# LSTM and three dense layers on one core: the last sixteen time steps as two portions of eight

## What is computed

```python
xW = einsum('ntd,dg->ntg', x, Wx) + b          # n=32, t=64, d=256, g=1024
def step((h, c), xw_t):
    a = xw_t + h @ Wh                          # Wh 256 x 1024
    i, f, o = sigmoid(a[:, :768] in three);  g = tanh(a[:, 768:])
    c = f * c + i * g
    h = o * tanh(c)
hs = scan(step)                                # 64 steps, one after the other
y = s0 * ([hs, -hs] @ pm1(k0))                 # 512 -> 1024
y = s1 * ((relu(y) * 2) @ pm1(k1))             # 1024 -> 1024
y = s2 * ((relu(y) * 2) @ pm1(k2))             # 1024 -> 256
out = x + y
```

## Time and profile before

| | |
|---|---|
| median of three runs | 282.81 us |
| the profiled execution | 282.9 us |
| its span (first to last instruction) | 281.1 us |
| TensorE busy | 275.7 us (98%) |
| VectorE busy | 203.1 us (72%) |
| ScalarE busy | 158.3 us (56%) |
| TensorE's granted clock | full in every slice |

### The profile page before, as it was taken

The page is one execution under the profiler, slowest core; times in us unless marked ns, Lnnn a source line. Parts: engine busy times, 40 slices in busy tenths (PEclk is TensorE's granted clock), DMA queues, the critical chain, the costliest instruction groups (busy, mean ns, idle before and its releaser), DMA issues.

```text
span 281.1 us, 8774 instructions
## 1 busy us (share of the span) xinstructions
PE 275.7 (98%) x3608; PEld 223.5 (80%) x3608; DVE 203.1 (72%) x747; ACT 158.3 (56%) x480; POOL 2.3 (1%) x10
## 2 busy tenths in 40 slices
PE   8899999999999999999999999999999999999995
PEld 5688888777998989999899999999999895544441
DVE  2787888887788888887888888788887875431113
ACT  5596987787656556565555566655566454211100
POOL 0100000000000000000000000000000000000000
PEclk9999999999999999999999999999999999999999
DMA  6960000000000001000100010000000100010001
GB/s 191 398 277 1 3 2 0 2 3 0 2 2 3 3 2 40 2 2 3 40 1 2 3 40 2 2 2 22 22 2 2 40 3 0 0 37 2 0 0 75
DMA packets 4791, 8.72 MB, mean 31 GB/s; under 512 B 912, under 2 KB 2448, under 8 KB 4624
## 3 DMA queue, kind: packets, MB, share of 16 engines
q1 hardware_dynamic: 4176, 7.87, 7.8%
q10 hardware_dynamic: 576, 0.30, 0.4%
HBM read 6.07 MB, written 2.10 MB: 29 GB/s over the span
## 4 chain that ended last, share of the span: by engine, by line
PE 90%; DVE 3%; DMA 3%; ACT 1%; SPq 1%; issue 0%; DVEq 0%
PE WK L396 48%; PE WK L379 14%; PE G L359 10%; PE ACC L409 9%; PE G L350 9%; DMA xw<-in_wh 3%; ACT tT L543 1%; DVE h L592 1%; DVE x L597 1%; DVE mx L574 0%; DVE aT L703 0%; SPq L315 0%; ACT tC L548 0%; DVE cD L714 0%; DVE uT L712 0%
## 5 line engine op out<-in xcount | busy, mean ns | idle before, releaser
L396 PE MATMUL WK<-h,k 128*128 128x256 f16 (+1 forms) x992 | 126.7, 276 | 0.1
L396 PEld LDWEIGHTS WK<-h,k 128*128 128x128 fp8e5 x992 | 93.6, 98 | 15.5 <-issue 1.6
L543 ACT ACTIVATE tT<-aT 128x128 f32<-128x128 f32 x126 | 39.0, 310 | 57.8 <-DVE aT L703 56.5
L592 DVE SCALAR_TENSOR_TENSOR h<-WK,h 128x256 f16<-128x256 f32 (+1 forms) x104 | 42.4, 439 | 27.2 <-ACT h L504 27.2
L504 ACT ACTIVATE h<-WK 128x256 f16<-128x256 f32 (+1 forms) x104 | 37.1, 388 | 30.0 <-PE WK L396 29.8
L703 DVE TENSOR_REDUCE aT<-G 128x128 f32<-128x256 f32 x128 | 48.2, 418 | 6.8 <-PE G L359 5.9
L486 ACT ACTIVATE G<-xw 128x256 f32<-128x256 f32 x126 | 46.6, 370 | 0.0
L379 PE MATMUL WK<-xs,wxs 128*128 128x512 f32 x168 | 43.7, 403 | 0.7 <-DVE wxs L570 0.7
L359 PE MATMUL G<-h,w 128*128 128x64 f16 x1008 | 39.5, 192 | 0.0
L350 PEld LDWEIGHTS G<-h,w 128*128 128x128 f16 x1008 | 32.6, 96 | 6.3 <-DVE h L720 4.0
L409 PE MATMUL ACC<-h,k 128*128 128x256 f16 (+1 forms) x224 | 36.5, 288 | 0.1
(11 more groups left out here) (63 smaller groups left out, 132.8 us busy)
## 6 DMA issues: line engine op xcount, KB each, us to landing
x<-in_x SPq DMA_DIRECT2D x3, 512.0 KB, 8.9
out_y<-x SPq DMA_DIRECT2D x12, 128.0 KB, 1.8
xw<-in_wx SPq DMA_DIRECT2D x4, 256.0 KB, 5.9
xw<-in_wh SPq DMA_DIRECT2D x4, 256.0 KB, 7.0
k<-in_k SPq DMA_DIRECT2D x1, 1024.0 KB, 10.8
k<-in_k SPq DMA_DIRECT2D x1, 512.0 KB, 8.3
out_y<-x SPq DMA_DIRECT2D x2, 256.0 KB, 2.0
x<-in_x ACTq DMA_DIRECT2D x1, 256.0 KB, 4.3
```

The source lines that it names most:

```text
L396: ins = eng.matmul(layer_src(tile), w, rhs, start=a == 0, stop=last)
L543: eng.activation(tT[:, B * j0:B * j1], aT[:, j0:j1].rearrange("p j b -> p (j b)"), ACT.Tanh, scale=half_gain0 if t == 0 else half_gain).th ...
L592: eng.scalar_tensor_tensor(layer_dst(tile, 1), layer_src(tile), 0.0, layer_dst(tile, 0), ALU.max, ALU.subtract).then_inc(lo_made[tile[0]])
```

## The change

`CHUNKS` gets eight portions of 8 steps in place of six of 8 and one of 16. `third` is called for every portion, so that the first-layer tiles of portions 6 and 7 stand beside the second-layer tiles of portions 5 and 6 as those of the earlier portions do, and the special order for the last portion goes. The first-layer outputs of portions 6 and 7 share the space of the former portion 6, half each, and the rule of when ScalarE may write there is extended to both.

```diff
-LAST = 2
-CHUNKS = ((0, 8), (8, 8), (16, 8), (24, 8), (32, 8), (40, 8), (48, 16))
+CHUNKS = ((0, 8), (8, 8), (16, 8), (24, 8), (32, 8), (40, 8), (48, 8), (56, 8))
@@ tile_order
-            if c < NC - 2:
-                order += third(c, m)
-        if c == NC - 2:
-            rest = [(tile, 1) for tile, n in order[-LAST:] for _ in range(n)]
-            del order[-LAST:]
-            share = len(rest) // 8
-            for n in range(8):
-                order += [((0, c + 1, n), 4)] + rest[share * n:share * n + share]
-            order += rest[8 * share:]
+            order += third(c, m)
     return order + [(("o", NC - 1, k), 2) for k in (6, 7, 6, 7)]
@@ lstm_ffn
         h1s = [f.rearrange("p (m a c) -> p m a c", m=8, a=2) for f in (
-            h1[:, 0:4096], h1[:, 4096:8192], h1[:, 0:4096], h1[:, 4096:8192], h1[:, 0:4096], h1[:, 4096:8192], h1b)]
+            h1[:, 0:4096], h1[:, 4096:8192], h1[:, 0:4096], h1[:, 4096:8192], h1[:, 0:4096], h1[:, 4096:8192], h1b[:, 0:4096], h1b[:, 4096:8192])]
@@ layer_hi
-                if layer == 0 and 2 <= c < NC - 1:
+                if layer == 0 and 2 <= c < NC - 2:
                     e.wait_ge(l_mm[1], 8 * (c - 1))
-                if layer == 0 and c == NC - 1:
+                if layer == 0 and c >= NC - 2:
                     e.wait_ge(seeded[1], 16)
```

## The result

The changed kernel takes 283.22 us (median of 22 runs, 282.56 to 283.90); the kernel before took 282.70 beside it (22 runs, 282.14 to 283.20). The ratio is 1.0020, with a 95% interval of 1.0013 to 1.0026: slower by 0.57 us, between 0.37 and 0.74 (the medians alone differ by 0.52). The forecast was 283.0 us, and 282.4 to 283.7 as the range.

The account below looks back on a forecast made before the run. The prediction took the kernel as bound by the columns TensorE streams, plus late steps and the end. Its terms, 1.73 + 0.17 - 1.47 - 0.2 = +0.23 us, gave 283.0 us, with 282.4 to 283.7 as the 8-in-10 range.

Parts of the forecast that it names:

- What bounds the kernel: Whole kernel: the columns TensorE streams, plus some tenths where a step is late, plus the end; no gap in 44.96 us.
- Two narrow for a wide: Last portions' matmuls: 192 wide become 384 narrow at 0.1091 us, +0.46; stretch after the last step +1.73 us.
- The straight line between the two spacings: TensorE matmul price: 81 ns at 128 columns and 131 at 512 give 98 at 256, costing 12.5 us; prediction rejected it.
- Steps 59 and 60: VectorE's queue: three pieces behind each step put h 3.52 us apart, so step 62 starts late, +0.17 us.
- from step 62 on h needs 3.12 again and is early: Steps from 62: h comes every 3.12 us again, so TensorE does not wait for it there.
- Behind the last step: Filling after step 63: no gap to win; banks return in 2.73 us against about 1.0 of emptying; cost nothing.
- B: Behind the last step: banks come back late, ten tiles wait 0.20 us each, +2.0, to 285.0 us; chance 0.08.
- E: Long narrow streams run slower than the fills: each 0.01 us more is 3.8 us, 286.8 us; chance 0.02.
- The end: From the last twelve output matmuls on: smaller pieces win back 1.47 us, the smaller last transfer 0.2 us.
- A: Steps with three VectorE pieces cost nearly nothing, 0.04 us each: 282.8 us; chance 0.13.
- C: Small terms at upper bounds: narrow at 0.1094 (+0.13), transfer unchanged (+0.2), steps +0.25: 283.4 us; chance 0.12.

## Why the prediction was right, and where it was short

- *What bounds the kernel.* Right: the stretch from the last step to the last twelve output matmuls is a count of matmuls, 46.72 us for a forecast of 46.69, and TensorE waits nowhere in it.
- *Two narrow for a wide.* Forecast 0.46; measured alone 0.45 for 360, so 0.48 for 384. The straight line between the two spacings of the Trainium skill ("TensorE: Matmul & The Clock Gate", section "Back-to-back issue gap") would have asked for an estimated 12.5 us; the traces don't agree, with 216 ns at 512 columns and 109 at 256.
- *Steps 59 and 60.* The mechanism was right and its first part exact: the h of steps 60 and 61 were forecast for 222.15 and 225.67 and are there then (221.93 and 225.45, each 0.22 long), and step 62 was forecast at 225.72 and stands at 225.74. The term of 0.17 was too small. The step of the reasoning that failed is "from step 62 on h needs 3.12 again and is early": the low part of the h of step 61 was not early, a stall of VectorE's own fell on the float32 h that it is made from, and TensorE waited 0.14 us within step 62. The whole term is 0.32 to 0.33 us: step 60 to step 63 takes 10.35 to 10.36 in three traces of the changed order and 10.03 before. No row of before shows it at step 61, but the idle 0.47 of step 22 stood in the trace, and I had not looked for such rows.
- *Behind the last step.* Nothing was lost and nothing won, as forecast; rivals B and E did not occur.
- *The end.* Forecast -1.67, measured -1.62 in the span: from the last twelve to the next matmul that waited there were 1.10 us, for 1.04. The gap behind the six covering matmuls, 0.44 us, is real and closed when ten covered. The transfer is shorter by 0.23 us in the span (2.27 for 2.50), for -0.2 forecast; but the forecast took the time outside the span as unchanged, and there it grew by about as much on average.
- *The rivals.* A (the crowded steps cost nearly nothing) holds for the first of the two, which cost 0.04 (3.31 us to step 61), and fails for the second (3.53 to step 62). C is the nearest to what came, but not by its terms: narrow cost 0.1091 and the transfer was shorter.
- *The forecast as a whole* has the direction and the parts right, and half of the size: +0.45 us in the trace for +0.23 forecast, with 0.14 missing for the stall, 0.05 at the end and 0.03 in the stretch. The timed loss of 0.57 is more than twice the forecast one, and the term that it had not looked at is the one outside the span. That 283.22 us lies so near to the forecast 283.0 is in part luck: the kernel before was timed at 282.70 this time and not at 282.81, and counted from there the forecast is 0.3 low. The 0.71 for a change within 0.2% is neither won nor lost: the ratio of 1.0020 lies on that border.

## What to carry to other kernels

Where an engine is full, as TensorE is here, cutting its work finer costs its price (here 1.2% of what was cut) and pays at the end alone, where the last emptying, the last y piece and its transfer are smaller; but less work is left to cover that emptying, so count the matmuls that cover it before and after. When tiles are moved into a loop with a recurrence, count the instructions that each engine holds ahead of the recurrence's next one: two steps in a row with three were costlier than the one with three before. And when starts vary from run to run, compare traces from the first instruction of the loop; waits of 0.1 us in a single step can then be read, which the times don't part. Take beside it the time outside the span for every execution: a change can move that too.

## What the runs showed of the hardware

VectorE stalled at two fixed places of its instruction stream, by 0.14 to 0.25 us, and in the same place in every trace of the same stream: at step 22 (0.47 us idle ahead of the high part in place of 0.22, in nine traces) and at step 61 (0.28 for 0.14, in three). With one instruction more ahead of them the one at step 61 fell one instruction earlier, and the one at step 22 was no longer seen. On the path of the recurrence such a stall was paid, with 0.12 us at step 22 and 0.14 at step 61. The granted clock reads 9 tenths or more in every slice of both pages; from step 0 to the last matmul it was at its upper level, 2.4 GHz, in both kernels, so it has no part in the difference.

The time outside the span has two levels with eight portions and one with the portion of 16, as given in the section on the result. In the ten traces the upper level (2.24 us and more) goes with an instruction transfer of 8 KB on q14 behind the end of the span.
